# The last four tiles of a pairwise-product kernel, gathered in two halves and moved together

## The reference

```
embed = tables[jnp.arange(FIELD_NUM)[None, :], sparse_inputs]      # 2048 x 26 x 32
p = jnp.einsum('bfe,bge->bfg', embed, embed)
l_z = jnp.einsum('bfe,feh->bh', embed, w_z)
l_p = jnp.einsum('bfg,fgh->bh', p, w_p)
l_1 = jax.nn.relu(jnp.concatenate([l_z + l_p + l_b, dense_inputs], axis=-1))
h = jax.nn.relu(l_1 @ W1 + b1)
return jax.nn.sigmoid(h @ Wf + bf)
```

## Time and profile before

| | |
|---|---|
| timed, median of 3 runs | 597.75 us (597.61 to 599.56) |
| the profiled execution, its own time | 600.24 us |
| its span, first to last instruction | 598.4 us |
| instructions in the trace | 1661 |
| POOL busy | 436.1 us (416 gathers: 424.9 us) |
| DVE (VectorE) busy | 418.2 us |
| ACT (ScalarE) busy | 140.2 us, 332 instructions |
| PE (TensorE) busy | 141.2 us |

### The profile page before, as it was taken

How to read it: one execution, slowest core, us unless ns; L and a number is a source line. 1 busy time by engine, 2 the same in 40 slices (tenths; PEclk the granted TensorE clock), 3 DMA queues, 4 the chain that set the end, 5 groups by cost and what they waited for, 6 DMA issues and landing times.

```text
span 598.4 us, 1661 instructions
## 1 busy us (share of the span) xinstructions
PE 141.2 (24%) x196; PEld 49.5 (8%) x196; DVE 418.2 (70%) x245; ACT 140.2 (23%) x332; POOL 436.1 (73%) x425
## 2 busy tenths in 40 slices
PE   0000000531242210503114510504024310062146
PEld 0000000210010000201001100201001100021011
DVE  4103599989901399989951379998980369998970
ACT  0000016033211125123222113403422210523042
POOL 6777777777777777777777777777777777777830
PEclk9999999856655755856556655675566655575667
DMA  6122322221122221211122222121111222112100
GB/s 144 13 14 13 13 13 13 14 13 14 13 13 13 13 14 12 11 12 11 12 12 12 12 12 12 11 13 12 12 11 11 13 11 12 12 11 12 31 11 1
DMA packets 19448, 9.50 MB, mean 16 GB/s; under 512 B 9824, under 2 KB 19437, under 8 KB 19437
## 3 DMA queue, kind: packets, MB, share of 16 engines
q0 software_dynamic: 13312, 6.84, 19.6%
q1 hardware_dynamic: 6126, 2.57, 1.8%
HBM read 8.85 MB, written 0.01 MB: 15 GB/s over the span
## 4 chain that ended last, share of the span: by engine, by line
issue 41%; DVE 30%; POOL 22%; ACT 3%; PE 1%; DMA 1%; DVEq 0%; ACTq 0%
POOL rows L259 22%; DVE prod L308 19%; DVE pairs L326 9%; DVE rows_T L336 2%; DMA rows<-in_L_rec_tables,which 1%; ACT field_rows L425 1%; ACT pair_rows L448 1%; PE ps_h L570 1%; PE ps_h L551 1%; ACT pair_rows L436 0%; DVE pair_rows L359 0%; DMA raw<-in_r_sparse_inputs 0%; ACT ps_copy L414 0%; ACT pair_rows L458 0%; ACT scores L482 0%
## 5 line engine op out<-in xcount | busy, mean ns | idle before, releaser
L259 POOL DMA_INDIRECT rows<-in_L_rec_tables,which x416 | 424.9, 1021 | 136.2 <-issue 133.7
L308 DVE TENSOR_TENSOR prod<-ps_copy,rows 128x1664 f32<-128x1664 f32 (+12 forms) x103 | 194.4, 1914 | 103.5 <-issue 101.5
L326 DVE TENSOR_REDUCE pairs<-prod 128x76 f32<-128x2432 f32 (+7 forms) x72 | 197.0, 2742 | 0.4 <-issue 0.4
L536 PE MATMUL ps_h<-field_rows,wz 128*128 128x512 f32 x96 | 63.3, 820 | 275.0 <-issue 234.5
L551 PE MATMUL ps_h<-pair_rows,w_pair 96*128 96x512 f32 (+2 forms) x64 | 53.8, 1004 | 140.3 <-issue 118.9
L425 ACT COPY field_rows<-rows_T 32x512 f32<-32x512 f32 (+1 forms) x112 | 58.8, 525 | 77.1 <-issue 67.1
L414 ACT COPY ps_copy<-rows 128x128 f32<-128x128 f32 (+2 forms) x59 | 20.7, 351 | 170.3 <-DMA rows<-in_L_rec_tables,which 158.3
L448 ACT COPY pair_rows<-pairs_T 32x256 f32<-32x256 f32 (+1 forms) x96 | 33.6, 350 | 96.8 <-issue 71.1
L336 DVE STREAM_TRANSPOSE rows_T<-rows 128x512 f32<-128x512 f32 (+1 forms) x28 | 18.5, 662 | 49.3 <-DMA rows<-in_L_rec_tables,which 49.0
L536 PEld LDWEIGHTS ps_h<-field_rows,wz 128*128 128x128 f32 x96 | 24.6, 267 | 315.2 <-issue 272.5
L551 PEld LDWEIGHTS ps_h<-pair_rows,w_pair 96*128 96x128 f32 (+2 forms) x64 | 18.6, 310 | 171.8 <-issue 148.8
(11 more groups left out here) (23 smaller groups left out, 24.6 us busy)
## 6 DMA issues: line engine op xcount, KB each, us to landing
rows<-in_L_rec_tables,which POOLq DMA_INDIRECT x416
wz<-in_L_rec_w_z SPq DMA_DIRECT2D x1, 768.0 KB
field_rows<-rows_T SPq DMA_DIRECT2D x16, 32.0 KB
w_pair<-in_w_low SPq DMA_DIRECT2D x1, 288.0 KB
w_back<-in_w_high SPq DMA_DIRECT2D x1, 288.0 KB
raw<-in_r_sparse_inputs SPq DMA_DIRECT2D x1, 156.0 KB, 2.3
w<-in_L_rec_W SPq DMA_DIRECT2D x1, 128.0 KB
dense_in<-in_r_dense_inputs SPq DMA_DIRECT2D x1, 104.0 KB
```

The lines of the kernel that those rows point to most:

```text
L259: nc.gpsimd.indirect_dma_start(rows[:, r % 2, f, k, :], None, table_rows, bass.IndirectOffsetOnAxis(ap=which[:, t, f:f + 1], axis=0),).the ...
L308: ins = nc.vector.tensor_tensor(products(n, s)[:, 0:tiles, at:at + g + 1, :], own.broadcast_to([P, tiles, g + 1, E]), rows[:, r % 2, 0:g + ...
L326: nc.vector.tensor_reduce(pairs[:, :, first:end], products(n, s), AX.X, ALU.add).then_inc(summed, 1)
L536: ins = nc.tensor.matmul(ps_h0[:, h, :], wz[:, j, h * P:(h + 1) * P], field_rows[:, j, :, :, :].rearrange("p q t b -> p (q t b)"), start=( ...
```

## The change

The last round is cut into two steps of two tiles each, so the kernel has five steps: rounds 0 to 2 as they were, step 3 (tiles 12 and 13) and step 4 (tiles 14 and 15). Each step of two tiles has its own groups:

```diff
+STEPS = [(g, 0, 4) + WHOLE for g in range(3)]
+STEPS += [(3, 0, 2,
+           [(0, 8), (8, 16), (16, 20), (20, 23), (23, 26)],
+           [(0, 8), (8, 12), (12, 15), (15, 18), (18, 20), (20, 22), (22, 24), (24, 26)])]
+STEPS += [(3, 2, 4,
+           [(0, 8), (8, 12), (12, 14), (14, 16)] + [(f, f + 1) for f in range(16, 26)],
+           [(0, 8), (8, 12), (12, 14), (14, 16)] + [(f, f + 1) for f in range(16, 26)])]
...
-    SP_MOVE = 1
+    SP_CHUNKS = [(0, 4), (4, 5)]
...
+    POOL_TILES = 1
```

The turned blocks of both steps are moved together, after step 4 has turned them. SyncE moves chunks 0 to 3, chunk 4 and the rows of chunk 6:

```diff
+            for m, (first, end) in enumerate(SP_CHUNKS):
+                sp.wait_ge(rows_turned, CH * LAST_STEP + end)
+                sp.wait_ge(lz_summed, MOVED * (r - 1) + end)
+                for q in range(QUADS):
+                    for u in range(PER):
+                        sp.dma_start(field_rows[Q * u:Q * (u + 1), first:end, q, :, :].rearrange("p c k b -> p c (k b)"),
+                                     rows_T[Q * q:Q * (q + 1), first:end, u, :, :].rearrange("p c k b -> p c (k b)"))\
+                            .then_inc(rows_moved[m], DMA)
+
+            sp.wait_ge(rows_turned, CH * (LAST_STEP + 1))
+            sp.wait_ge(lp_summed, (TAIL + 1) * r)
             for q in range(QUADS):
...
+                for u in range(LAST):
+                    sp.dma_start(pair_rows[Q * u:Q * (u + 1), TAIL, q, :, :].rearrange("p k b -> p (k b)"),
+                                 rows_T[Q * q:Q * (q + 1), MOVED, u, :, :].rearrange("p k b -> p (k b)"))\
+                        .then_inc(last_rows_moved, DMA)
```

ScalarE moves chunk 5 and all pairs; its list for the last two steps:

```diff
+            r = ROUNDS - 1
+            lay_last_pairs(r - 1)
+            make_hidden0(r - 1)
+            for u in range(len(STEPS[r][3])):
+                copy_fields(r, u)
+                if u == 0:
+                    make_hidden1(r - 1)
+                if u == 1:
+                    make_scores(r - 1)
+            lay_last_pairs(r)
+            for u, (first, end) in enumerate(STEPS[LAST_STEP][3]):
+                if first != STEPS[LAST_STEP][4][POOL_STAGE][0]:
+                    copy_fields(LAST_STEP, u)
+                if 20 <= first < 23:
+                    lay_pairs(r, 0, first - 20)
+            for q in range(QUADS):
+                lay_rows(r, 1, q)
+            for u in range(PLACES):
+                lay_pairs(r, 1, u)
+            lay_last_pairs(LAST_STEP)
             make_hidden0(ROUNDS - 1)
             make_hidden1(ROUNDS - 1)
-            make_scores(ROUNDS - 1)
+            for p in range(HALVES):
+                make_scores_part(p)
```

The end of the last round is cut in halves of 256 columns: the second layer goes into two banks, ScalarE makes one half of hidden1 and VectorE the other, and there are two logits and two sigmoids. The first half of hidden0 waits for the first of TAIL's two matmuls alone (`half_summed`):

```diff
+            def sum_h1_parts():
+                for h in range(HALVES):
+                    if h:
                         pe.wait_ge(half_made, 1)
                     else:
...
+                        pe.wait_ge(hidden0_made, HALVES * (ROUNDS - 1) + 1)
+                    for p in range(HALVES):
+                        bank = ps_end if p else ps_h1
+                        ins = nc.tensor.matmul(bank[:, 0:PART], w1[:, h, :], hidden0[:, h, PART * p:PART * (p + 1)],
+                                               start=False, stop=(h == HALVES - 1))
+                        if h == HALVES - 1:
+                            ins.then_inc(h1_summed, 1)
```

More of the change, by code:

```diff
@@ L84, in chunk_rows, with unit_of @@
         return E * chunk_fields(j)
-    def unit_of(f):
-        return next(u for u, (first, end) in enumerate(UNITS) if first <= f < end)
+    def unit_of(i, f):
+        return next(u for u, (first, end) in enumerate(STEPS[i][3]) if first <= f < end)
     def move_of(j):
@@ new lines, in add_up, with turn_rows @@
+                nc.vector.tensor_reduce(pairs[:, k0:k1, first:end], products(i, s), AX.X, ALU.add).then_inc(summed, 1)
+            def turn_rows(i, j):
+                group, k0, k1, units, stages = STEPS[i]
+                n = chunk_fields(j)
+                for u in range(unit_of(i, PER * j), unit_of(i, PER * j + n - 1) + 1):
+                    has_landed(dve, i, u)
+                if group and k0 == 0:
+                    dve.wait_ge(rows_laid, NM * (group - 1) + move_of(j) + 1)
+                nc.vector.transpose(rows_T[:, j, 0:n, k0:k1, :].rearrange("p f k b -> p f (k b)"),
+                                    rows[:, group % 2, PER * j:PER * j + n, k0:k1, :].rearrange("p f k e -> p f (k e)"))\
@@ L404, in _, with copy_fields @@
         @block.scalar
         def _(act):
-            def copy_fields(r, u):
-                first, end = UNITS[u]
-                n = NU * r + u - COPIES
+            def copy_fields(i, u):
+                g, k0, k1, units, stages = STEPS[i]
+                first, end = units[u]
+                n = UNITS_TO[i] + u - COPIES
                 if n >= 0:
-                    act.wait_ge(multiplied, NS * (n // NU) + stage_of(UNITS[n % NU][1] - 1) + 1)
-                act.wait_ge(landed[r][u], DMA * K * (end - first))
-                nc.scalar.copy(ps_copy[:, (NU * r + u) % COPIES, 0:end - first, :, :],
-                               rows[:, r % 2, first:end, :, :]).then_inc(copied, 1)
+                    before = next(b for b in range(len(STEPS)) if n < UNITS_TO[b + 1])
+                    last = STEPS[before][3][n - UNITS_TO[before]][1] - 1
+                    act.wait_ge(multiplied, STAGES_TO[before] + stage_of(before, last) + 1)
+                has_landed(act, i, u)
+                nc.scalar.copy(copies(i, u), rows[:, g % 2, first:end, k0:k1, :]).then_inc(copied, 1)
@@ L573, in sum_logit, with sum_logit_part @@
+            def sum_logit_part(p):
+                if p:
+                    pe.wait_ge(part_made, 1)
+                else:
+                    pe.wait_ge(hidden1_made, ROUNDS)
+                    pe.wait_ge(multiplied, STAGES_TO[LAST_STEP + 1] - 1)
+                nc.tensor.matmul(ps_copy[0:1, p, 0:PART], wf[:, :], hidden1[:, PART * p:PART * (p + 1)], start=True, stop=True)\
+                    .then_inc(logit_made, 1)
             def sum_logit(r):
@@ L583, in _ @@
                     sum_lp(r, c)
-                first, end = MOVES[1]
-                for j in range(first, end - 1):
+                sum_dense(r)
+                for j in range(*MOVES[1]):
                     sum_lz(r, j)
```

311 lines of the change are left out of this document (174 added, 137 removed).

## The result

The changed kernel took **608.62 us** (median of 4 runs, 608.36 to 609.50), the kernel before 598.65 (597.61 to 599.76) beside it: ratio 1.0174 [1.0154, 1.0194], about 10 us slower. The forecast was 630. The sign was right and the size three times too large. The profiled execution took 608.36 us, its span is 606.6.

What follows compares the result with a forecast made beforehand. ScalarE's 48 tail copies, held to one per 1.40 us, were taken to bound it: 620.7 for the last, plus 8.2 and 3.6, gives 632.5 on the profile's clock, about 630 us timed; range 616 to 640, with rivals 588 to 642.

Steps and rivals of the forecast that it cites:

- the rule's last part: Engines' issue: after the free dozen, one instruction per 1.40 us; the last of ScalarE's 48 tail copies ends at 620.7.
- free dozen: Engines' issue: after a rest, about a dozen instructions go at their own pace (SyncE about four).
- VectorE's second stage of step 3: VectorE, first two tiles of the last round: starts at 485 us, behind hidden1 and the second copy.
- step 3's end: VectorE's products and sums for two tiles, from 485 us: ends at 535.8.
- SyncE's start: SyncE's 40 issues start when chunk 3 is turned, about 551 us, and end at 603.7.
- VectorE's end: VectorE's work left behind t0 (fields 21 to 25) ends at about 591 us, against 579.8 before.
- t0: Step 4 (last two tiles): pairs of fields 0 to 19 turned at 570 us, where ScalarE's 48 tail copies begin.
- rival C: VectorE held at 1.4 us per instruction too, to the full: t0 at 573 to 574, time 634 us; chance 0.07.
- Rival B: ScalarE let through faster, SyncE's queue last: rows at 604.2, timed 613.5 us; chance 0.10.
- Rival A: Pace of 1.4 us absent from timed runs, or from ScalarE and SyncE: 583.5 us, 2.4% faster; chance 0.20.
- some 9 us left: In Rival A, VectorE's work behind the last gather (about 564 us), so it ends at 573.
- The unknown of hidden1: Why hidden1 came 7.9 us after its matmul; if it no longer does, t0 up to 8 us earlier, time 622.

Runs made afterwards that it cites:

- h1: Kernel before without the last round's 104 gathers, on a held chip: 565.42 us against 598.89.
- e12: Changed kernel with ScalarE copying field 21 ahead of the first pair copies, on a held chip: 609.11 us, ratio 1.0178 to the kernel before.
- f1: Changed kernel unaltered, on a free chip: 551.74 us against 561.08 for the kernel before, ratio 0.9819.
- e3: Changed kernel with ScalarE's field copies of the last stages ahead of the first pair copies, free chip: 553.39 us, ratio 0.9847 to the kernel before.
- e4: Changed kernel with SyncE moving chunks 0 to 4 in one set of 16 DMAs instead of two, free chip: 555.78 us, ratio 0.9898 to the kernel before.
- g4: Changed kernel with ScalarE copying field 21 ahead of the first pair copies, on a free chip: 549.34 us against 560.95 for the kernel before, ratio 0.9782.
- e2: Kernel before with POOL waiting ahead of the third round's gathers for VectorE's last product of the second, free chip: 584.0 us, ratio 1.0408.
- f3: Kernel before with POOL waiting ahead of the third round's gathers for VectorE's last product of the second, another set, free chip: 583.38 us.
- g2: Kernel before with POOL waiting ahead of the third round's gathers for VectorE's last product of the second, a third set, free chip: 584.8 us.
- e11: Kernel before with 16 needless SyncE DMAs (12288 pieces) in the third round, held chip: 600.5 us in one run, kernel before 596.6 to 599.5.
- f4: Kernel before, unaltered, run again for its profile on a held chip: 597.17 us.

## Why the prediction was right or wrong, by its steps

**The step that failed** is the rule's last part, "from then on one per 1.40 us", carried to the end: "The last starts at 570 + 36 x 1.40 = 620.4". The free dozen and the pace were real, and the formula fits up to copy 22 of 48; but the pace ends at 589.3, and the other 26 take 8 us. The last copy ended at 597.07 instead of 620.7: 23.6 of the 24.1 us by which the sum on the profile's clock (632.5) lay above the 608.36 measured. The runs put in its place a debt of the gathers common to the engines, which ends at about 3.7 + 416 x 1.40 us with the number of gathers taken from h1 and with ScalarE's list in another order in e12. In before the last held copy started at 585.55, so its rows could not show the end; but that POOL itself slows only between the 49 and the 43 of the earlier trace rows was a sign of something that fills. With the end of the hold taken from the trace: 589.3 + 26 copies of 0.3 = 597, the hidden layer and the end behind it, 608.

**Why the change loses on a held chip at all.** The prediction had both parts of it, but gave nearly all to ScalarE's copies. First, VectorE is done later: its last turn ends at 593.5, before at 579.8. The changed kernel has the first copies of the round behind the hidden layers of the round before, and these are held (hidden1 at 484.51), so VectorE's second stage starts 11 us later against the last gather than in f1. Second, what is left for ScalarE and SyncE is moved in the hold and right behind it. As an estimate: from the last sum to the end of the span it is 9.5 us in f1, where nothing is held; 592.1 + 9.5 = 601.6 would be 3.2 us above the 598.4 of before, and the 5.0 us from there to 606.6 are the queues. That split is read off rows; no run on a held chip has those copies placed earlier. In e12 VectorE ended 1.3 us sooner and nothing was gained, which fits the queues being last.

**The steps that held.** VectorE's second stage of step 3 at 485.7 (485), step 3's end at 535.0 (535.8), SyncE's start at 550.3 (551) and its 32 issues in 40.74 (by the forecast's terms 4 x 0.75 + 28 x 1.38 = 41.6), VectorE's end at 593.5 (591). t0 came at 573.7 instead of 570; 3.02 us of it is "issue" ahead of the turn of the pairs, which is absent in f1 (sum until 521.51, turn at 521.54). That looks like rival C in a small way, VectorE held too; no run tests it.

**Rival B's mechanism was the last link**, by some 2 us: SyncE's rows came at 592.3, TensorE worked off 16 matmuls until 600.9, the last four of which needed ScalarE's last copy (597.07) and stood at about 599.1. Only 3.9 us lay from there to the scores at 604.77. I had B at 604 and 0.10, with the same failed term (eight issues at 1.38; they took 0.62 each).

**Rival A** (583.5 of 597.75, 2.4% faster, 0.20) had the sign and about the size on every free chip on which the changed kernel or a variant of it ran: 1.8% in f1, 1.0 to 2.2% in e3, e4 and g4. Its condition never came up as written: it kept POOL's gathers at 1.40 us, and on free chips they too go at 1.25. I argued against it with the 1.40 of POOL in the timed runs. That was true of that chip and said nothing about others. (The 1.22 us that the argument used for an unheld gather is a count in a window; the gathers themselves start 0.95 + 0.30 = 1.25 apart, which makes its 30 us some 28 and changes nothing.) Its "some 9 us left" for VectorE behind the last gather were 16.3: the pairs of fields 0 to 19 were turned only at 521.5, under three us ahead of the last gather's end, so VectorE's sum and not the gathers bound step 4.

**The unknown of hidden1** (7.9 us) belongs to the hold: in h1, where the hold is over, ScalarE waits 1.01 us for that matmul, and in the changed kernel hidden1 comes at 484.51 as before.

**Open**: what is owed. All runs here, timed ones too, list span and clock of the core, so none was without the hardware profiler's records. The Trainium skill ("NOTIFIC — the notification-queue block", section "7.1 Overflow: three behaviours, one of which stalls the engine") says that the block that writes such records holds its producers back rather than lose one inside; its section "10. Constraints, capacities, measured rates" says that an implicit record costs the engine zero cycles. A debt common to all engines would fit the first and not the second, and neither says why chips would differ; no run here shows which records a gather makes, or a kernel without them. So whether a plain run on a held chip is held stays open, too. Not tried on a held chip: the gathers spaced out, and a change in the number of instructions of the other engines, which would tell a debt of the gathers from a debt of all instructions.

## What to carry to other kernels

Time a change on more than one chip before its sign is believed: the same two kernels gave +1.7% and -1.8%, and the sign could be read from one row, the distance between instructions that wait for nothing ("issue" at 1.4 us against 0.3). Where engines are held so, look for what is owed (number of the slowest kind of instruction x its held distance) and when it is paid: work placed behind that point goes at its own pace, and work ahead of it does not. Where nothing is held, what counts is how much data-bound work is left behind the last gather, and TensorE's backlog comes next.

## What the runs showed of the hardware

- The same kernel takes 598 us on chips 0, 1 and that of the first set and 561 on 6, 7, 10 and 14, each numbered one met in one set. Its 416 gathers, or those of the changed kernel, end at 561 to 563 us on chip 1 and that of the first set and at 523 to 524 on the others, except where POOL was made to wait (e2, f3, g2); chip 0 ran no profile with 416.
- On the held ones copies (0.30 us) start about 1.40 apart, SyncE's issues take 1.27 on average over 32 (1.38 from the fifth of 16 on) instead of 0.62 to 0.71, and it ends for both at 589.3 in the changed kernel.
- The hold stops 26 to 28 us behind the last gather (440.8 for 312 gathers, 588.8 to 589.3 for 416). With 12288 more DMA packets the last gather ended 2.0 us later than without (e11, f4).
